# Zeroing the blocks of the cross keys by DMA, and epsilon as the bias of the square roots

## What is computed

```
q_c  = rms_norm(x @ wq_down.T);  kv_c = rms_norm(x @ wkv_down.T)     # eps 1e-6
a    = latent attention(q_c, kv_c, rope), causal, 16 heads @ wo.T
x1   = layernorm(x + a)                                              # eps 1e-5
qp   = x1 @ Wq.T;  k, v = split(ctx @ Wkv_expand.T)                  # 16 heads of 32
c    = softmax(causal(qp k^T / sqrt(32))) v @ Wout.T
x2   = layernorm(x1 + c)
y    = shared experts(x2) + top-2 of 16 routed experts(x2)
out  = layernorm(x2 + y)
layernorm(x) = (x - mean) / sqrt(var + eps)
```

## Time and profile before

| | us |
|---|---|
| median of 3 runs (902.88 to 906.53) | 903.31 |
| the profiled execution, its own time | 902.72 |
| its span in the trace | 900.9 |
| TensorE busy | 838.2 |
| VectorE busy | 528.1 |
| ScalarE busy | 474.8 |
| GpSimd busy | 240.8 |

### The profile page before, as it was taken

How to read it: one execution, slowest core, us unless ns; L and a number is a source line. 1 busy time by engine, 2 the same in 40 slices (tenths; PEclk the granted TensorE clock), 3 DMA queues, 4 the chain that set the end, 5 groups by cost and what they waited for, 6 DMA issues and landing times.

```text
span 900.9 us, 13299 instructions
## 1 busy us (share of the span) xinstructions
PE 838.2 (93%) x4302; PEld 710.2 (79%) x4302; DVE 528.1 (59%) x979; ACT 474.8 (53%) x1225; POOL 240.8 (27%) x278
## 2 busy tenths in 40 slices
PE   6978999999999987889998789999999999999997
PEld 5766888788788775777776678888888988889896
DVE  3553753654664557666767755636465665656467
ACT  5514752743753554676576651525473745637150
POOL 0222230132132021455455100431232332321420
PEclk9989999999999998999999999999999999999999
DMA  8022315133322400321222020543464564653432
GB/s 324 1 78 63 123 43 157 65 99 98 123 85 55 146 21 21 84 49 38 55 52 67 2 71 24 183 166 119 146 206 164 187 199 153 198 166 131 137 94 82
DMA packets 39486, 96.33 MB, mean 107 GB/s; under 512 B 15824, under 2 KB 21840, under 8 KB 37808
## 3 DMA queue, kind: packets, MB, share of 16 engines
q1 hardware_dynamic: 28384, 57.95, 20.6%
q0 software_dynamic: 11056, 37.79, 12.9%
HBM read 71.59 MB, written 20.97 MB: 103 GB/s over the span
## 4 chain that ended last, share of the span: by engine, by line
PE 62%; issue 15%; DVE 8%; ACT 7%; POOL 4%; SPq 1%; DMA 1%; POOLq 0%; ACTq 0%; DVEq 0%
PE ps L1490 50%; ACT Pt L829 3%; PE ps L1505 3%; PE ps L1830 2%; POOL Pt L593 2%; PE ps L1820 1%; PE ps L1550 1%; PE ps L1640 1%; DVE negmax L1101 1%; SPq L514 1%; DVE acc L1117 1%; PE ps L1711 1%; PE ps L1832 1%; DVE kb L1218 1%; DVE stats L1123 1%
## 5 line engine op out<-in xcount | busy, mean ns | idle before, releaser
L593 POOL TENSOR_TENSOR Pt<-Pt,rowinv 112x448 f32<-112x448 f32 x64 | 59.9, 936 | 226.6 <-DVE rowinv L1108 226.2
L829 ACT ACTIVATE Pt<-ps,negmax 112x112 f32<-112x112 f32 x256 | 87.2, 356 | 49.1 <-DVE negmax L1101 49.0
L1490 PE MATMUL ps<-x2T_hi,ws_hi 128*128 128x448 f32 x256 | 96.0, 375 | 4.3 <-DVE x2T_lo L1030 4.3
L1490 PE MATMUL ps<-x2T_lo,ws_hi 128*128 128x448 f32 x256 | 94.2, 368 | 0.0
L1490 PE MATMUL ps<-x2T_hi,ws_lo 128*128 128x448 f32 x256 | 94.1, 368 | 0.0
L1490 PE MATMUL ps<-w_hi,h_hi 128*128 128x512 f32 x224 | 89.9, 401 | 0.0
L957 ACT ACTIVATE hf<-ps,b 128x448 f32<-128x448 f32 x64 | 40.6, 635 | 92.3 <-PE ps L1490 72.9
L1490 PE MATMUL ps<-w_hi,h_lo 128*128 128x512 f32 x224 | 88.5, 395 | 0.0
L1490 PE MATMUL ps<-w_lo,h_hi 128*128 128x512 f32 x224 | 88.4, 395 | 0.0
L1030 DVE TENSOR_TENSOR h_lo<-hf,h_hi 128x448 fp32r<-128x448 f32 x64 | 39.9, 623 | 48.7 <-ACT h_hi L958 47.9
L1374 DVE TENSOR_TENSOR acc<-ps,acc 128x512 f32<-128x512 f32 x56 | 38.6, 689 | 44.4 <-PE ps L1490 35.4
(11 more groups left out here) (282 smaller groups left out, 2248.6 us busy)
## 6 DMA issues: line engine op xcount, KB each, us to landing
stage<-in_wf SPq DMA_DIRECT2D x30, 513.0 KB
rows_in<-in_zeros SPq DMA_DIRECT2D x30, 256.0 KB, 4.0
xs<-rows_in POOLq DMA_DIRECT2D x29, 256.0 KB, 4.3
rows_out<-yb POOLq DMA_DIRECT2D x29, 256.0 KB
stage<-in_wa SPq DMA_DIRECT2D x4, 1408.0 KB, 6.6
stage<-in_wb SPq DMA_DIRECT2D x4, 1280.0 KB, 5.6
qr<-ro_hi SPq DMA_DIRECT2D x64, 56.0 KB, 2.0
qr<-ro_lo SPq DMA_DIRECT2D x64, 56.0 KB, 2.0
```

Source lines behind the costliest of these rows:

```text
L593: nc.gpsimd.tensor_tensor(p, p, rowinv[0:S, b % 2, :].unsqueeze(2).broadcast_to([S, GH, S]), ALU.mult).then_inc(norm_done, 1)
L829: last = nc.scalar.activation(Pt[0:S, b % 2, h * S:(h + 1) * S], ps[0:S, b % 2, h * S:(h + 1) * S], ACT.Exp, bias=negmax[0:S, b % 2, h:h + 1],
L1490: ins = mm(dst, w, x, start=start and i == 0, stop=stop and i == len(ops) - 1, skip_group_check=not (start and stop))
```

## The change

Three edits.

1. The four KB steps leave VectorE's list. GpSimd zeroes a new tile kz of 128 x 448 numbers in iteration 3 of its list (KZ), and SP fills kb from it by four DMAs, each of which reads a row of kz four times over. They are issued after the load of cx, once `a_free["G"]` says that the last G step is copied. The semaphore `kb_zero` becomes one for each half, and each spread waits for its own.
2. The roots of the RMS norm and of the three layer norms read the variance (ss or mv) itself and take epsilon as a bias from a tile eps, which GpSimd fills at the start; VectorE's additions and their semaphores go, and ScalarE waits for `sq_done` or `ln_mv`.
3. ScalarE waits at the start for three of GpSimd's small memsets instead of one.

```diff
@@ lists
 ATT_LAST_DVE = weave(range(8), [("Z", 2), ("S", 0), ("T", 1), ("N", 0), "fill"], fill={
-    **_last, 5: [("KB", 0), ("W", 2), ("KB", 1)], 6: [("KB", 2), ("KB", 3), ("W", 3)],
+    **_last, 5: [("W", 2)], 6: [("W", 3)],
-ATT_LAST_POOL = weave(range(8), _pool, fill={5: [("CX",)], 6: [("LK",)], 7: [("L",)]})
+ATT_LAST_POOL = weave(range(8), _pool, fill={3: [("KZ",)], 5: [("CX",)], 6: [("LK",)], 7: [("L",)]})
@@ SP
             sp.dma_start(cx[:, :, :], d["ctxT"][:, :, 0:S]).then_inc(cx_ld, 16)
-            sp.wait_ge(kb_zero, 2)
+            sp.wait_ge(kz_set, 1)
+            sp.wait_ge(a_free["G"], NG * B)
+            for half in range(2):
+                for a in range(2):
+                    sp.dma_start(f32(kb[:, half, a, :, :, :]).rearrange("p b h s -> p b (h s)"),
+                                 f32(kz[:, :]).unsqueeze(1).broadcast_to([P, HB, GH * S])).then_inc(kb_zero[half], 16)
+            sp.wait_ge(kb_zero[0], 32)
             spread_keys(0, 0)
 ...
-            sp.wait_ge(kb_zero, 4)
+            sp.wait_ge(kb_zero[1], 32)
             spread_keys(0, 1)
@@ GpSimd
             nc.gpsimd.memset(one[:, :], 1.0).then_inc(one_set, 1)
+            nc.gpsimd.memset(eps[:, 0:1], RMS_EPS).then_inc(one_set, 1)
+            nc.gpsimd.memset(eps[:, 1:2], LN_EPS).then_inc(one_set, 1)
...
+                elif kind == "KZ":
+                    nc.gpsimd.memset(f32(kz[:, :]), 0.0).then_inc(kz_set, 1)
@@ ScalarE
-            act.wait_ge(one_set, 1)
+            act.wait_ge(one_set, 3)
...
-                act.wait_ge(eps_done, r + 1)
-                nc.scalar.activation(ss_root[0:S, HB * r:HB * r + HB, :],
-                                     ss_eps[0:S, HB * r:HB * r + HB, :], ACT.Sqrt).then_inc(root_done, 1)
+                act.wait_ge(sq_done, HB * r + HB)
+                nc.scalar.activation(ss_root[0:S, HB * r:HB * r + HB, :], ss[0:S, HB * r:HB * r + HB, :], ACT.Sqrt,
+                                     bias=eps[0:S, 0:1]).then_inc(root_done, 1)
...
-                act.wait_ge(ln_eps, ln_part(i, r) + 1)
-                nc.scalar.activation(rstd[:, lo:hi], rstd[:, lo:hi], ACT.Sqrt).then_inc(ln_root, 1)
+                act.wait_ge(ln_mv, ln_part(i, r) + 1)
+                nc.scalar.activation(rstd[:, lo:hi], mv[:, lo:hi, 1], ACT.Sqrt, bias=eps[:, 1:2]).then_inc(ln_root, 1)
@@ VectorE
-                dve.wait_ge(sq_done, HB * r + HB)
-                nc.vector.tensor_scalar(ss_eps[0:S, rows, :], ss[0:S, rows, :], RMS_EPS, None, ALU.add)\
-                  .then_inc(eps_done, 1)
...
-                dve.wait_ge(ln_mv, part)
-                nc.vector.tensor_scalar(rstd[:, lo:hi], mv[:, lo:hi, 1], LN_EPS, None, ALU.add)\
-                  .then_inc(ln_eps, 1)
...
-                elif kind == "KB":
-                    dve.wait_ge(a_free["G"], NG * B)
-                    dst = kb[:, j // 2, j % 2, :, :, :]
-                    nc.vector.memset(f32(dst).rearrange("p b h s -> p (b h s)"), 0.0).then_inc(kb_zero, 1)
...
-                dve.wait_ge(ln_mv, LN_ALL + t + 1)
-                V.tensor_scalar(rstd[:, t:t + 1], mv[:, t, 1:2], LN_EPS, None, ALU.add).then_inc(ln_eps, 1)
```

More of the change, by code:

```diff
@@ L298, in build @@
         one = sb("one", [P, 1])
+        eps = sb("eps", [P, 2])
         warm = sb("warm", [P, 1])
@@ L327, in build @@
         ss = sb("ss", [P, B, 2], at=first)
-        ss_eps = sb("ss_eps", [P, B, 2], at=first)
         ss_root = sb("ss_root", [P, B, 2], at=first)
@@ L375, in build @@
         kb = sb("kb", [P, 2, 2, HB, GH, S], F32R, xat)
+        held.append(2 * 2 * HB * GH * S)
+        gap("over_kr", 38136)
+        kz = sb("kz", [P, GH * S], F32R, xat)
         xat.close()
@@ L435, in build @@
         yg_ld = [sem(f"yg_ld{i}") for i in range(4)]
-        (const_done, in_hi, in_lo, down_done, sq_done, eps_done, root_done, rinv_done, nat_done,
+        (const_done, in_hi, in_lo, down_done, sq_done, root_done, rinv_done, nat_done,
          kvn_hi, kvn_lo, tr_done, tr_hi, tr_lo, kr_done, kr_mul, kr_rot, krh, krl) = map(sem, (
-            "const_done in_hi in_lo down_done sq_done eps_done root_done rinv_done nat_done kvn_hi "
+            "const_done in_hi in_lo down_done sq_done root_done rinv_done nat_done kvn_hi "
             "kvn_lo tr_done tr_hi tr_lo kr_done kr_mul kr_rot krh krl").split())
@@ L450, in build @@
             "pt_free z_done z_hi z_free rot_add rot_hi rot_lo").split())
-        (ln_stat, ln_mv, ln_eps, ln_root, ln_inv, ln_minus, ln_row, ln_out, lt_done, lt_hi, lt_lo) = map(sem, (
-            "ln_stat ln_mv ln_eps ln_root ln_inv ln_minus ln_row ln_out lt_done lt_hi lt_lo").split())
-        kb_zero, cxs_hi, cxs_lo, zs_hi, zs_lo = map(sem, "kb_zero cxs_hi cxs_lo zs_hi zs_lo".split())
+        (ln_stat, ln_mv, ln_root, ln_inv, ln_minus, ln_row, ln_out, lt_done, lt_hi, lt_lo) = map(sem, (
+            "ln_stat ln_mv ln_root ln_inv ln_minus ln_row ln_out lt_done lt_hi lt_lo").split())
+        kb_zero = [sem(f"kb_zero{half}") for half in range(2)]
+        kz_set, cxs_hi, cxs_lo, zs_hi, zs_lo = map(sem, "kz_set cxs_hi cxs_lo zs_hi zs_lo".split())
         (fw_hi, fw_lo, up_done, gelu_done, h_lo_done, y_done, y_free) = map(sem, (
@@ L1021, in _ @@
             for t in range(TT):
-                act.wait_ge(ln_eps, LN_ALL + t + 1)
-                nc.scalar.activation(rstd[:, t:t + 1], rstd[:, t:t + 1], ACT.Sqrt).then_inc(ln_root, 1)
+                act.wait_ge(ln_mv, LN_ALL + t + 1)
+                nc.scalar.activation(rstd[:, t:t + 1], mv[:, t, 1:2], ACT.Sqrt, bias=eps[:, 1:2]).then_inc(ln_root, 1)
         @block.vector
@@ L1126, in variances @@
                 lo, hi = LN_PARTS[i][r]
-                part = ln_part(i, r) + 1
                 dve.wait_ge(ln_stat, TT * i + hi)
```

## The result

| | before | after |
|---|---|---|
| median, us | 903.1 (902.07 to 906.53, 4 runs) | 896.29 (895.91 to 897.38, 4 runs) |
| ratio | | 0.992, 95% interval 0.9892 to 0.9948 |
| span of the profiled execution | 900.9 | 894.1 |

The kernel became 6.8 us faster by these medians. Two later measurements of the same pair, with more executions, gave 5.9 and 6.3 us (902.11 to 896.21 and 901.53 to 895.2), so the gain is about 6 to 7 us. The sum was made for one execution (902.7 less 7.5); the profiled execution after took 895.91 us.

A forecast was written before the change was run, and what follows sets the result against it. VectorE's in-order queue with kb's memsets paces the seam before cross attention; TensorE bounds the last stage. 7.1 − 0.09 + 0.44 + 0.08 = 7.5 us, so 902.7 − 7.5 = 895.2 us; range 892.8 to 898.6.

The forecast's parts named there:

- The memsets: Seam before cross attention: four kb memsets, 6.2 us of VectorE's in-order queue, lie on the path and delay TensorE.
- W3: TensorE's output product at the seam: starts 2.7 us sooner, at 337.2, and takes 2.8 us at full clock.
- the exponentials of batch 7: ScalarE at the seam: they start at 342.7 instead of 348.16, 5.5 us sooner.
- The stalled addition: Layer norm 1's root follows the warm-up without VectorE's 1.973 us epsilon addition: 0.7 us more, less 0.09 for the bias.
- The minus instruction held by GpSimd: Layer norm at the seam: VectorE's new minus, with two SBUF inputs, waits for GpSimd's read, adding 0.05 us.
- W5 at full clock: TensorE behind the turns: W5 and three products take 3.5 us instead of 4.47, giving back 0.9 us.
- rival 1: Clock falls despite shorter gaps, W3 and W5 slow as before: total gain 5.1 us, 897.6 us; chance 0.20.
- The first scores: Cross attention's first score product starts at 363.5 instead of 370.66, waiting for qx_lo and not for a DMA.
- The zeros: Four DMAs zeroing kb take 14.7 us from 334.7 to 349.4, covered by 11 us: cost nothing.
- Rivals 2 and 3: Late kb zeros: 899.5 us at 120 GB/s, chance 0.05; slower than before below 110 GB/s, chance 0.04.
- The other roots: Epsilon as bias at four further places on the path: 0.11 us each, 0.44 us; layer norm 2's first part 0.08.
- later stages start sooner by the same amount: Everything behind the seam keeps its order and waits, so the whole gain of 7.5 us stays.

The follow-up runs named there:

- kz_only: Kernel before with only the first edit: kb zeroed by GpSimd's KZ and four DMAs, epsilon still added by VectorE; 897.67 us, ratio 0.9961.
- eps_only: Kernel before with only epsilon as bias of the roots, kb still zeroed by VectorE; 899.92 us, ratio 0.9993.
- zeros3: Changed kernel with the DMAs that zero kb issued three times over, spreads waiting for the last pass; 901.03 us in one run.
- after_again: Changed kernel measured a second time, code unaltered; 896.21 us, ratio 0.9943 to the kernel before.
- after_3: Changed kernel measured a third time, code unaltered; 895.2 us, ratio 0.9932 to the kernel before.
- before_again: Kernel before measured a second time, code unaltered; 903.09 us in one run.
- v0_early: Changed kernel with the value projection V 0 (twelve products) moved ahead of the turns of the first normalised rows; 895.88 us, ratio 0.9934.
- v0_fill: Changed kernel with projection V 0 ahead of the turns and ten idle products ahead of cross attention's first scores; 894.24 us, ratio 0.9907.
- v0_fill_2: Same program as v0_fill, measured again beside the changed kernel; 894.39 us, ratio 0.9918 to the kernel before.

## Why the prediction was right, and where it was not

**The memsets were on the path: right.** W3 at 2.69 us against 2.7, the exponentials of batch 7 at 5.34 against 5.5. kz_only shows the same move alone: 5.33 us at the root. W3's twelve products took 3.04 us against 2.8 summed (in before they lay between 339.93 and 344.34); the clock in 336 to 340 is 1.00, as the forecast had it.

**The stalled addition: right.** The forecast had the root 0.5 us sooner by it; eps_only measured 0.68 with the memsets still there. The two edits together give the 6.00 that was summed, since this 0.18 too much makes up for the memsets' 0.17 too little. The forecast let the root start at the end of the warm-up (0.20 us); in after it starts 0.11 us behind the warm-up's start. The bias was charged 0.09 us. The seven roots of the last layer norm, which follow no warm-up, give it, before and after (duration in ns, min/median/max):

```profile
L1023 ACT ACTIVATE rstd<-rstd x7: 202/203/205, 879.3 to 897.5; 128x1 f32<-128x1 f32 x7
```

```profile
L1037 ACT ACTIVATE rstd<-mv,eps x7: 294/294/294, 872.4 to 890.6; 128x1 f32<-128x1 f32 x7
```

That is 0.091 us. The Trainium skill (ScalarE: Activation LUTs, "What ACT_TABLE_LOAD costs") says about 93 ns for a per-partition operand; the traces agree within 0.002 us. Only the root at the seam, close behind the warm-up, shows 0.08. The bound of "0.085 us at most" was a little low.

**The minus instruction held by GpSimd: not at the seam.** It started at 345.87, while GpSimd's wx_lo (344.67 + 1.28 = 345.95) was still at work, and took its usual 0.16 us, which reach 0.08 us beyond that end; there was nothing left to hold. The same instruction in layer norm 2 starts 0.10 us behind the start of a GpSimd instruction, in all thirteen traces, those of the kernel before too. In after:

```profile
494.10 0.29 DVE L1149 SCALAR_TENSOR_TENSOR minus<-mv,rstd 128x4 f32<-128x4 f32 x1
```

```profile
494.00 0.37 POOL L608 TENSOR_TENSOR zx_hi<-zf,one 128x112 fp32r<-128x112 f32 x1 [3.77 <-DVE zf L1254]
```

It takes 0.29 us and ends 0.02 us behind GpSimd's instruction. The Trainium skill (SBUF — State Buffer, "Who interferes with whom") says that an instruction with two SBUF inputs contends with a GpSimd instruction that reads SBUF; these traces agree. VectorE's addition of epsilon took long in both kernels that have it, 1.973 us in before and 1.98 in kz_only.

**W5 at full clock: the step that failed.** "I take that 0.9 as given back, since 1.3 us is nearer to the 1.55 than to the 2.08." In the trace after, it was not given back but 0.69 us more was lost: 1.66 us off. The runs show that no such comparison could decide it. The gap was as foreseen (1.21 us), and with it the program has 5.16, 3.65 and 5.04 us, and 5.19 in zeros3 (gap of 1.23). With a gap of 1.97 kz_only has 5.13, with 1.34 eps_only has 3.65, and with 2.08 the kernel before has 4.47. It should have been a chance between 3.65 and about 5.1 us, with rival 1 heavier than its 0.20; of rival 1 the half on W5 occurred, the half on W3 in none of the traces with the first edit. Filling the gap brings W5 to 3.65 us, so idleness is part of the cause; why the clock holds in one execution and falls in the next stays open.

**The first scores: a term left out.** The forecast spoke of W5 alone. Yet TensorE is slow at the first scores and the turns behind them in before as well, and not in after. A copy of ScalarE behind both places, before and after:

```profile
381.44 0.55 ACT L755 ACTIVATE qx_hi<-ps 128x448 fp32r<-128x448 f32 x1 [1.33 <-PE ps L1490]
```

```profile
374.02 0.55 ACT L769 ACTIVATE qx_hi<-ps 128x448 fp32r<-128x448 f32 x1 [1.44 <-PE ps L1491]
```

From the first scores to here the lead grows from 6.28 to 7.42 us, 1.1 us given back that no step had. It hid the greater part of the miss at W5, and it was luck: after_again and after_3, the same program, fell here and were given back nothing. Counted from the mark, at this copy after is 6.6 us ahead (slow at W5 alone), after_3 5.6 (slow at both places) and after_again 7.0 (slow at the scores alone), against a forecast of 7.0.

**The zeros: right, with a price too high.** 0.115 us a piece was taken as an upper bound, 14.7 us in all; they took about 9.9 us, 0.078 us a piece for each of the 16 engines. They ended at 344.8, not 349.4. Rivals 2 and 3 needed 140 GB/s or less, and 370 came.

**The other roots: right where they can be read.** From the last tile's row 890.58 and 0.30 us, and the end, the way from the last product to the last instruction's end is 2.77 us against 2.87: 0.10, forecast 0.11. It is within 0.01 us the same in all ten traces with the edit, and as before in kz_only and before_again. The RMS norm can be read by itself as well, from the leads just ahead of and behind its second half (ScalarE's copies at 37.5 and 41.1 us of before): 0.11 to 0.12 us in the ten traces with the edit, 0.00 in kz_only and before_again, forecast 0.11. Layer norm 2 can't, since falls of the clock lie around it.

**The balance.** Spans: 0.78 us lead at the mark, 5.50 at the first scores, 1.1 by 381 us, 0.5 lost behind (7.42 to 6.90): 6.8 to 6.9 us. The forecast's 7.5 and this agree to 0.6 us, but in part because misses cancel: -1.66 at W5 against +1.1 at the first scores and +0.78 from the start of the program. So the nearness of the median to the forecast is partly luck. The 0.5 us behind 381 us goes against "later stages start sooner by the same amount". It is no chance: between 381 and 450 us every trace with a changed seam loses 0.4 to 0.6 us of its lead, before_again 0.1. A longer wait for later spreads is part of it (TensorE waits 0.69 us for `kb<-kx` at 423.58 in after, 0.28 at 430.49 in before); the rest stays open. Behind 450 us falls of the clock add to it: between 381 and 531 us the three traces of the changed kernel gave -0.7, +1.3 (after_again) and +1.1 us (after_3) against the same trace of before.

## What to carry to other kernels

Memsets in the in-order queue that the critical path runs through cost nearly their own time: four of 1.55 us, 6.2 in all, held the seam back by 5.3 us. Four DMAs from a small cleared tile do the same work in 10 us where no engine notices, if the first reader is further away than that. Replay the stretch with measured durations and each engine's order, and here it came out within 0.2 us; but book clock given back as a chance and not as a term, and look for every stretch in which the clock is low, not for the first alone. To compare two traces, count from a common instruction ahead of the change, and take more than one trace of the changed kernel.

## What the runs showed of the hardware

- The granted clock behind one and the same gap differs between executions of one program: 15 products in 5.16, 3.65 and 5.04 us behind gaps of 1.2 us. In the traces of v0_early and v0_fill the clock was 0.66 and 0.67 over 76 to 84 us, in the first attention group, and they stand 2.9 to 3.0 us behind at the mark; v0_fill_2, the program of v0_fill, had 1.00 there and stands 0.3 us ahead. Part of the scatter of whole runs seems to be this: of the eight of after_again the fastest two have 894.55 and 894.58 us at a mean clock of 0.993, the slowest two 898.82 and 899.58 at 0.987 and 0.988; the four between don't follow the clock strictly (895.54 to 896.91 at 0.987 to 0.993).
- Five unused products of 512 columns in the gap before the turns, or a projection moved there, left W5 at 3.64 to 3.65 us in all five traces; ten before the first scores left them and the turns behind at full pace in all three. Without filling, both places came out slow in some executions and at full pace in others.
- DMAs from a 128 x 448 tile to kb within the chip's own memory ran at 370 GB/s in pieces of 1792 B, 0.078 us a piece for each engine. The packing of qr in pieces of the same size spent at most 0.115 us on each.
- A bias tile on a root of one column costs 0.091 us (0.294 against 0.203).
- An instruction of VectorE with two inputs, held by GpSimd, shows no wait but becomes longer itself: 0.29 us instead of 0.16.
